# A two-layer graph network on one core: eleven counted groups move from layer 0 to the end of it and into layer 1

## The chip, the core and the metric

The kernel runs on one core of a Trainium2 chip. Its engines run side by side, each through its own list of instructions, and meet at semaphores: PE (TensorE) multiplies matrices into PSUM, DVE (VectorE) and ACT (ScalarE) work on elements, POOL (GpSimd) and SP (SyncE) issue DMAs, and ACT issues some too. The metric is the device time of one execution in microseconds (us); less is better.

## The reference

There are 6250 nodes with 128 features and 100000 edges, sorted by their destination. One layer, applied twice, is

```python
msg = (h[src] + edge_feats) @ Wn.T
agg = segment_sum(msg, dst, num_segments=num_nodes)
agg = agg / maximum(deg, 1.0)[:, None]
self_msg = where(iso[:, None], h @ Wi.T, h @ Ws.T)      # iso = deg == 0
x = agg + self_msg
h_next = where(x >= 0, x, RRELU_SLOPE * x)
```

Both layers have the same edges and edge features, and weights of their own. The result is the layer norm of `x + h` over the features.

## The kernel before, in words

The sum over a node's edges is taken before the product with `Wn`. The edges stand in 784 chunks of 128. Four chunks are a window, whose destinations lie within 40 columns; 16 chunks are a group, whose destinations lie within 136. There are 196 windows and 49 groups. The layer's sums lie in SBUF as `sums`, features by nodes.

*Edge features* are needed once: layer 1 starts from layer 0's sums, and adds only the difference that `h` makes. They are loaded window by window (SP, five windows ahead) and multiplied with a one-hot matrix `onehot` of the destinations, into `ps_win`. In two windows of five DVE first splits the features into three bf16 parts (`split_feats`), and PE multiplies three times in bf16 in place of once in f32.

*Source rows* `h[src]` come in one of two ways.
- Gathered: POOL issues one indirect DMA per chunk, in order, up to five windows (`ROWS`) ahead of PE (`gather`). PE multiplies the three bf16 parts of the rows with the one-hot matrix. All windows of groups that are not counted go this way.
- Counted: for a group, a matrix `counts` (nodes by 136 columns) says how often each node is the source of an edge into each column. It is multiplied with all nodes' parts `h_parts`: 49 tiles x 3 parts = 147 products. To make it, DVE writes for each chunk two one-hot matrices, `is_lane` and `is_code` (`make_codes`), six chunks ahead (`AHEAD`); PE multiplies them into a bank of `ps_count`, in two pieces of 294 and 343 columns and a small one of 49 (`count_piece`); ACT copies each piece from PSUM into one of three buffers of `counts` (`keep_chunk`).

32 of the groups are `KEEPABLE`; 31 of these are `KEPT`, counted for layer 1. 20 of the 31 are `USED`: counted in layer 0 too. The other 11 are gathered in layer 0, and counted only for layer 1. So in layer 0 two groups in three are gathered, but one in three where a second group is `USED` (the 7th, 19th, 31st and 43rd).

*Order.* Layer 0 runs in beats of one window. The plan `plan_layer0` deals two used groups and one other, and says how many chunks are counted in each beat and which tiles of a used group are multiplied. A full buffer is stored to DRAM by SP (`store_counts`, 1764 KB), for layer 1. `count_piece` goes round three banks, and waits for ACT's copy of the piece three before.

After a beat in which three groups are summed, a node step follows for 384 nodes: the products with the three weights, the activation, and `h` split into parts and stored in `h_parts_rows`. When all steps are through, SP loads `h_parts` back in seven cuts of seven tiles (`load_parts`), and POOL begins layer 1's gathers.

Layer 1 also runs in beats of a window: 72 windows are gathered. SP loads the 31 stored counts in seven cuts each, 217 loads of 252 KB, up to 21 ahead (`load_counts`). Per beat PE multiplies three or four cuts ("pieces", 21 products each, `multiply_kept`), then its window, then what is due of node steps. DVE adds the group's sums (`take_dense`) and the window's, and ACT stores the results.

The rows name what the products write: `ps_count` L1246 and L1250 are counts being made, `ps_dense` L1258 groups of layer 0 multiplied, `ps_count` L1258 those of layer 1 (they use the banks of `ps_count`), `ps_win` L1197 windows, `ps_self` L1310 and `ps_node` L1323 node steps.

Of the kernel before, what the change touches and what calls it, by code (L numbers as in the profile page):

```python
# [5 lines left out]
def plan_layer0(kept, used, beats, buffers, per_chunk, tiles, tiles_per_beat, head):  # L6
# [10 lines left out]
    total = len(jobs) * per_chunk  # L17
    builds, pieces, built = [], [], 0
    build_beat, done_beat = {}, {}
    waiting = [j for j, g in enumerate(jobs) if g in used]  # L20
    k, tile = 0, 0
    while built < total or waiting:
        now = []
        while len(now) < 4 and built < min(total, head + (k + 1) * (total - head) // beats):
            j = built // per_chunk
            if j >= buffers and jobs[j - buffers] in used and done_beat.get(j - buffers, k) >= k:
# [7 lines left out]
        if waiting and build_beat.get(waiting[0], k) < k:  # L34
            j = waiting[0]
            cut = (j, tile, min(tiles, tile + int((k + 1) * tiles_per_beat) - int(k * tiles_per_beat)))
            tile = cut[2]
            if tile == tiles:
                done_beat[j] = k
                waiting.pop(0)  # L40
# [3 lines left out]
    return jobs, builds, pieces, build_beat, done_beat  # L44


def gnn_resnorm_kernel(nc, x_rows, x_cols, src, dst, edges, wn0, ws0, wi0, wn1, ws1, wi1, out):
# [51 lines left out]
    JOBS, BUILDS, MULTIPLIED, BUILT_BEAT, DONE_BEAT = plan_layer0(KEPT, USED, 188, BUFFERS, GC, TILES, 5.6, 8)  # L99
    USED_JOBS = [j for j, g in enumerate(JOBS) if g in USED]  # L100
    FIRST_COL = {g: i * GC for i, g in enumerate(KEEPABLE)}
    COUNTED = len(KEEPABLE) * GC
    LAST_MULTIPLY = max(DONE_BEAT.values())

# [11 lines left out]
    PIECES = len(KEPT) * CUTS  # L116
    SPREAD = len(ORDER1) - GW
    PIECES1 = [min(PIECES, k * PIECES // SPREAD) for k in range(len(ORDER1) + 1)]


    READY = [[], []]
    for u in range(TRIOS):
# [5 lines left out]
        pieces = CUTS * sum(g < 3 * u + 3 for g in KEPT)  # L128
# [31 lines left out]
    with ctx:  # L160
# [108 lines left out]
        counts_loaded = [sem(f"counts_loaded{i}") for i in range(BUFFERS * CUTS)]  # L269
# [89 lines left out]
        def dense_bank(nth):  # L359

            if nth < len(USED):
                return ps_dense[:, 0, 0:WIDE]
            return ps_count[:, (nth - len(USED)) % BANKS, 0:WIDE]
# [14 lines left out]
        def _(sp):  # L378
# [59 lines left out]
            def load_counts(q):  # L438

                i, cut = divmod(q, CUTS)  # L440
                if q == 0:
                    sp.wait_ge(group_multiplied, len(USED))
                    for b in range(BUFFERS):
                        sp.wait_ge(counts_stored[b], 16 * len(JOBS[b::BUFFERS]))
# [3 lines left out]
                sp.dma_start(counts[:, i % BUFFERS, t, :].rearrange("p t s -> p (t s)"),  # L448
                             counts_kept[FIRST_COL[KEPT[i]] // GC, :, CUT * cut * SPAN:CUT * (cut + 1) * SPAN]
                             ).then_inc(counts_loaded[q % (BUFFERS * CUTS)], 16)  # L450
# [3 lines left out]
            with sp.If(flag == 0):  # L454
                cuts = list(range(CUTS))
                for k in range(BEATS[0]):
# [7 lines left out]
                    for j in range(len(JOBS)):  # L464
                        if BUILT_BEAT[j] == k - 1:
                            store_counts(j)
                    while cuts and k > max(LAST_MULTIPLY, WINDOWS) and (
                            READY[0][min(-(-P * (1 + CUT * (cuts[0] + 1)) // TRIO), TRIOS) - 1] + 7 <= k):
                        load_parts(cuts.pop(0))
                for q in range(CUTS):  # L470
                    load_counts(q)
# [3 lines left out]
                for q in range(CUTS, PIECES):  # L475
                    load_counts(q)
# [79 lines left out]
        def _(dve):  # L556
# [332 lines left out]
            def layer0():  # L889
# [9 lines left out]
                for k in range(BEATS[0]):  # L899
                    for j in USED_JOBS:  # L900
# [21 lines left out]

            def layer1():
# [5 lines left out]
                for k in range(1, BEATS[1]):  # L929
                    while added < PIECES1[min(k, len(ORDER1))] // CUTS:  # L930
                        dve.wait_ge(cut_multiplied, CUTS * (added + 1))
# [13 lines left out]
                    node_stage1(k)  # L945
# [523 lines left out]
```

## Time and profile before

| | |
|---|---|
| median of 3 runs | 1080.71 us (1080.55 to 1085.12) |
| the profiled execution | 1087.57 us, its span 1085.8 us |
| busy: PE, DVE, ACT, POOL | 933.4, 691.7, 513.5, 760.0 us |
| layer 0's gathers by POOL | 442, busy 450.9 us |
| layer 1's gathers by POOL | 286, busy 278.1 us |
| stores of counts | 31 of 1764 KB |
| loads of counts | 217 of 252 KB |
| mean granted TensorE clock | 0.960 |

The span runs from the profile's first instruction to the last. "Busy" of PE is the union of modelled times from start to end; products overlap, so what one costs in a stream is read from start to start. An instruction's idle time before it stands in brackets with what ended it; "issue" means that the engine waited for nothing that the profile shows.

### The profile page before, as it was taken

What the parts mean: (1) busy time and instruction counts of PE and PEld (TensorE: products, weight loads), DVE (VectorE), ACT (ScalarE), POOL (GpSimd) and SP (SyncE); (2) the same over time, 40 slices, a digit from 0 to 9 for tenths busy, and PEclk for the clock granted to TensorE, in tenths of its full rate; (3) what the DMA queues carried; (4) which work ended last, traced back from release to release, by engine and by line L of the source; (5) the groups of instructions that cost most, each with busy time, mean ns of one, the idle gap of its engine ahead of it and who ended that gap; (6) DMA issues with size and microseconds to landing.
All of it is one profiled execution on the core that took longest, in us unless ns stands there. A gap on an engine that the chain in (4) does not pass through costs nothing.

```text
span 1085.8 us, 38527 instructions
## 1 busy us (share of the span) xinstructions
PE 933.4 (86%) x14592; PEld 869.7 (80%) x14592; DVE 691.7 (64%) x2388; ACT 513.5 (47%) x1143; POOL 760.0 (70%) x757
## 2 busy tenths in 40 slices
PE   1599989899998998998889987479999999999982
PEld 0488888788988887887878886479999999998981
DVE  7878987898897898887878885312243233423333
ACT  6478777777887777776767774100000000000000
POOL 8367757777767777767777657077777777777772
PEclk9999999999999999998989998599999999999995
DMA  9468877878887797797778778799988898888741
GB/s 303 154 198 269 298 250 261 268 258 277 278 287 260 241 325 249 225 314 243 230 231 282 250 253 298 225 367 316 281 260 271 252 280 273 262 265 276 225 117 52
DMA packets 154041, 277.50 MB, mean 256 GB/s; under 512 B 21458, under 2 KB 112572, under 8 KB 149884
## 3 DMA queue, kind: packets, MB, share of 16 engines
q1 hardware_dynamic: 93504, 184.10, 50.5%
q0 software_dynamic: 35584, 72.92, 22.9%
q10 hardware_dynamic: 24764, 17.95, 5.2%
q8 instruction: 120, 1.97, 0.7%
q14 instruction: 69, 0.57, 0.2%
HBM read 202.58 MB, written 72.30 MB: 253 GB/s over the span
## 4 chain that ended last, share of the span: by engine, by line
PE 48%; issue 6%; DVE 4%; DMA 3%; ACT 2%; POOL 2%; ACTq 1%; DVEq 0%; SPq 0%; POOLq 0%
PE ps_count L1258 25%; PE ps_win L1197 7%; PE ps_dense L1258 6%; PE ps_count L1246 5%; PE ps_self L1310 3%; PE ps_node L1323 2%; POOL rows L512 2%; DMA rows<-x_parts_rows,idx 1%; ACT counts L1051 1%; DVE is_code L727 1%; DMA counts<-counts_kept 1%; PE ps_win L1204 1%; DMA h_parts_rows<-row_parts 1%; DVE is_lane L725 1%; PE ps_self L1292 0%
## 5 line engine op out<-in xcount | busy, mean ns | idle before, releaser
L512 POOL DMA_INDIRECT rows<-x_parts_rows,idx x442 | 450.9, 1020 | 189.0 <-issue 127.9
L1051 ACT CAST counts<-ps_count 128x294 f32 x992 | 436.4, 504 | 151.2 <-PE ps_count L1246 69.1
L512 POOL DMA_INDIRECT rows<-h_parts_rows,idx x286 | 278.1, 972 | 111.9 <-issue 84.8
L1246 PE MATMUL ps_count<-is_code,is_lane 128*128 128x294 bf16 x992 | 301.9, 311 | 35.3 <-ACT counts L1051 33.4
L1258 PE MATMUL ps_dense<-counts,h_parts 128*128 128x136 bf16 x2940 | 311.0, 224 | 3.9 <-DVE sums L760 2.2
L1258 PE MATMUL ps_count<-counts,h_parts 128*128 128x136 bf16 x4557 | 282.1, 223 | 10.0 <-DMA counts<-counts_kept 10.0
L1258 PEld LDWEIGHTS ps_count<-counts,h_parts 128*128 128x128 bf16 x4557 | 273.5, 98 | 10.7 <-DMA counts<-counts_kept 10.4
L1197 PE MATMUL ps_win<-onehot,feats 128*128 128x40 f32 (+1 forms) x1564 | 245.0, 236 | 22.9 <-DVE sums L738 11.3
L1258 PEld LDWEIGHTS ps_dense<-counts,h_parts 128*128 128x128 bf16 x2940 | 210.2, 98 | 39.7 <-ACT counts L1051 5.1
L1197 PEld LDWEIGHTS ps_win<-onehot,feats 128*128 128x128 f32 (+1 forms) x1564 | 205.9, 158 | 28.1 <-issue 19.9
L727 DVE TENSOR_SCALAR is_code<-codes,code 128x637 bf16<-128x637 f16 x496 | 197.9, 399 | 0.0
L1197 PE MATMUL ps_win<-onehot,rows 128*128 128x40 bf16 (+1 forms) x2224 | 149.0, 186 | 32.4 <-issue 29.6
L738 DVE TENSOR_TENSOR sums<-sums,ps_win 128x80 f32 (+1 forms) x268 | 59.1, 220 | 184.0 <-PE ps_win L1197 134.1
L1063 ACT COPY self_sums<-ps_self 128x384 f32<-128x384 f32 (+1 forms) x34 | 16.1, 475 | 321.7 <-PE ps_self L1310 321.7
L1197 PEld LDWEIGHTS ps_win<-onehot,rows 128*128 128x128 bf16 (+1 forms) x2224 | 130.3, 112 | 36.5 <-issue 33.4
L725 DVE TENSOR_SCALAR is_lane<-column,lane 128x128 bf16<-128x128 bf16 x496 | 135.9, 274 | 36.7 <-PE ps_count L1250 34.7
L1246 PEld LDWEIGHTS ps_count<-is_code,is_lane 128*128 128x128 bf16 x992 | 108.3, 110 | 46.1 <-ACT counts L1051 40.5
L1250 PE MATMUL ps_count<-is_before,is_lane 128*128 128x49 bf16 x465 | 88.7, 191 | 0.0
L697 DVE TENSOR_TENSOR onehot<-column,rel 128x160 f32<-128x160 bf16 x268 | 84.8, 318 | 1.6 <-issue 1.6
L712 DVE TENSOR_TENSOR feats<-feats_rest 128x512 bf16<-128x512 f32 x78 | 58.4, 749 | 2.7
L710 DVE TENSOR_TENSOR feats_rest<-feats 128x512 f32<-128x512 f32 x78 | 53.2, 682 | 6.6 <-DMA feats<-in_edges_dram 6.5
L1197 PE MATMUL ps_win<-onehot,feats_rest 128*128 128x40 bf16 x310 | 56.0, 182 | 0.0
(99 smaller groups left out, 784.7 us busy)
## 6 DMA issues: line engine op xcount, KB each, us to landing
counts_kept<-counts SPq DMA_DIRECT2D x31, 1764.0 KB
counts<-counts_kept SPq DMA_DIRECT2D x217, 252.0 KB, 4.4
feats<-in_edges_dram SPq DMA_DIRECT2D x196, 256.0 KB
rows<-x_parts_rows,idx POOLq DMA_INDIRECT x442
x_parts_rows<-h_parts SPq DMA_DIRECT2D x7, 672.0 KB, 7.7
h_parts<-h_parts_rows SPq DMA_DIRECT2D x7, 672.0 KB, 9.6
h_parts_rows<-row_parts ACTq DMA_DIRECT2D x16, 288.0 KB
rows<-h_parts_rows,idx POOLq DMA_INDIRECT x286
```

The costliest lines, as they stand in the source:

```text
L512: nc.gpsimd.indirect_dma_start(rows[:, SUB * slot + c, :], None, table[:, :], bass.IndirectOffsetOnAxis(ap=indices[:, c:c + 1], axis=0)).t ...
L697: nc.vector.tensor_tensor(onehot[:, h:h + SUB, :], column[:, 0:W].unsqueeze(1).to_broadcast([P, SUB, W]), rel[:, chunk:chunk + SUB].unsque ...
L710: nc.vector.tensor_tensor(rest, f, upper(f), ALU.subtract).then_inc(feats_rest_made, 1)
L712: nc.vector.tensor_tensor(lower(f), rest, upper(rest), ALU.subtract).then_inc(feats_split, 1)
L725: nc.vector.tensor_scalar(is_lane[:, n % (AHEAD + 1), :], column[:, :], lane[:, col:col + 1], None, ALU.is_equal)
L727: nc.vector.tensor_scalar(is_code[:, n % AHEAD, :], codes[:, :], code[:, col:col + 1], None, ALU.is_equal).then_inc(codes_ready, 1)
L738: return nc.vector.tensor_tensor(s, s, p, ALU.add)
L1051: nc.scalar.copy(counts[:, j % BUFFERS, :, at(offset + first, count)], ps_count[:, q % BANKS, 0:count * TILES].rearrange("p (r t) -> p t r ...
L1197: last = nc.tensor.matmul(ps[:, 0, SUM * w:(SUM + 1) * w], left, right, start=first and i == 0, stop=final and i == len(lefts) - 1)
L1246: last = nc.tensor.matmul(ps[:, 0:count * TILES], is_lane[:, n % (AHEAD + 1), :], is_code[:, n % AHEAD, first * TILES:(first + count) * TI ...
L1250: last = nc.tensor.matmul(ps[:, 0:TILES], is_lane[:, (n - 1) % (AHEAD + 1), :], is_before[:, (n // 4) % 3, n % 4, :], start=False, stop=True)
L1258: last = nc.tensor.matmul(bank, h_parts[:, t, k, :], counts[:, b, t, 0:WIDE], start=(t == 0 and k == 0), stop=(t == TILES - 1 and k == PAR ...
```

## The change

The eleven groups that only layer 1 uses leave the middle of layer 0. Jobs are ordered by `USED` first, then `LATE`. `plan_layer0` now plans the 20 used groups over 176 beats (before, 31 over 188). Two late groups are counted right after the last used one, two chunks per beat, until beat 191. The other nine are counted in layer 1, three chunks a beat at most, by a new plan `plan_layer1`. The late groups are not stored and not loaded: they lie in two buffers of `counts`, and are multiplied from there. The third buffer (`RING`) takes the 20 stored groups, one after another: 140 loads in place of 217; a cut is loaded when the same cut of the group before is multiplied. From the first late group on, counts are made in two banks of `ps_count`; the third bank and `ps_dense` take layer 1's groups in turn. Layer 1 begins with 14 pieces before its first window (before, three): two groups' first six cuts, then their last. The first seven loads are issued when the last features are. `SPLIT_RATE`, two windows in five, is the same number before and after.

```diff
-    plain = [g for g in kept if g not in used]
-    jobs, first = [], list(used)
-    while first or plain:
-        for some, count in ((first, 2), (plain, 1)):
-            jobs += some[:count]
-            del some[:count]
...
+def plan_layer1(order, late, built, beats, first, per_chunk, most):
+    chunks = late * per_chunk
+    ends, done, builds, upto, pos = {}, {}, [], [0], 0
+    for p in range(built // per_chunk):
+        ends[p] = -1
+    k = 0
+    while pos < len(order) or built < chunks:
+        target = first + max(0, (len(order) - first) * k // beats)
+        while pos < min(target, len(order)):
+            p, last = order[pos]
+            if p is not None and ends.get(p, k) >= k:
+                break
+            if p is not None and last:
+                done[p] = k
+            pos += 1
+        upto.append(pos)
+        now = []
+        while len(now) < most and built < chunks:
+            p = built // per_chunk
+            if p >= 2 and done.get(p - 2, k) >= k:
+                break
+            now.append(built)
+            built += 1
+            if built % per_chunk == 0:
+                ends[p] = k
+        builds.append(now)
+        k += 1
+    return upto, builds
...
-    JOBS, BUILDS, MULTIPLIED, BUILT_BEAT, DONE_BEAT = plan_layer0(KEPT, USED, 188, BUFFERS, GC, TILES, 5.6, 8)
+    LATE = [g for g in KEPT if g not in USED]
+    JOBS = USED + LATE
+    BUILDS, MULTIPLIED, BUILT_BEAT, DONE_BEAT = plan_layer0(len(USED), 176, BUFFERS, GC, TILES, 5.6, 8)
...
-    PIECES1 = [min(PIECES, k * PIECES // SPREAD) for k in range(len(ORDER1) + 1)]
+    PIECES = [(i, c) for i in range(2) for c in range(CUTS - 1)] + [(i, CUTS - 1) for i in range(2)]
+    PIECES += [(i, c) for i in range(2, len(KEPT)) for c in range(CUTS)]
...
+    PIECES1, BUILDS1 = plan_layer1(
+        [(LATE.index(KEPT[i]) if KEPT[i] in LATE else None, c == CUTS - 1) for i, c in PIECES],
+        len(LATE), 2 * GC, len(ORDER1) - GW, 2 * CUTS, GC, 3)
...
+    COUNT_BANK = [q % BANKS if q < LATE_COUNTS else q % 2 for q in range(COUNTS)]
...
-                if q >= BUFFERS * CUTS:
-                    sp.wait_ge(cut_multiplied, q - BUFFERS * CUTS + 1)
+                if l >= CUTS:
+                    sp.wait_ge(cut_multiplied, LOADED[l - CUTS] + 1)
...
+                    if k == max(LAST_MULTIPLY + 2, WINDOWS - FEATS):
+                        for l in range(CUTS):
+                            load_counts(l)
...
+            def make_late_codes(k):
+                for n in (BUILDS1[k] if k < len(BUILDS1) else ()):
+                    if n + AHEAD < len(JOBS) * GC:
+                        make_codes(n + AHEAD)
...
+                if j >= len(USED) + 2:
+                    act.wait_ge(cut_multiplied, LAST_PIECE[KEPT.index(JOBS[j - 2])] + 1)
...
                 for k in range(BEATS[1]):
+                    keep_chunks(BUILDS1[k] if k < len(BUILDS1) else ())
                     if (1, "self", k) in STAGE:
...
-                    while k < len(ORDER1) and q < PIECES1[k + 1]:
-                        multiply_kept(q)
-                        q += 1
+                    builds = BUILDS1[k] if k < len(BUILDS1) else []
+                    q, q1 = (2 * builds[0], 2 * (builds[-1] + 1)) if builds else (0, 0)
+                    s, s1 = PIECES1[min(k, len(ORDER1))], PIECES1[min(k + 1, len(ORDER1))]
+                    while q < q1 or s < s1:
+                        if q < q1:
+                            count_piece(q)
+                            count_piece(q + 1)
+                            q += 2
+                        if s < s1:
+                            multiply_piece(s)
+                            s += 1
```

In PE's list, at the end of layer 0's last node step (`ps_node<-ident`) and the start of layer 1, there stood before (L1258 are pieces, x63 three of them, L1197 a window):

```order
L1310 MATMUL ps_self<-wts,h_in 128x128
L1323 MATMUL ps_node<-wts,sums 128x128 x2
L1333 MATMUL ps_node<-ident,h_row 128x128 x2
L1258 MATMUL ps_count<-counts,h_parts 128x136 x63
L1197 MATMUL ps_win<-onehot,rows 128x40 x12
```

and now (L1341 are pieces, L1280 a window, L1329 counts being made):

```order
L1412 MATMUL ps_node<-wts,sums 128x128 x2
L1422 MATMUL ps_node<-ident,h_row 128x128 x2
L1341 MATMUL ps_dense<-counts,h_parts 128x136 x126
L1341 MATMUL ps_count<-counts,h_parts 128x136 x126
L1341 MATMUL ps_dense<-counts,h_parts 128x136 x21
L1341 MATMUL ps_count<-counts,h_parts 128x136 x21
L1280 MATMUL ps_win<-onehot,rows 128x40 x12
L1329 MATMUL ps_count<-is_code,is_lane 128x294
L1329 MATMUL ps_count<-is_code,is_lane 128x343
L1341 MATMUL ps_dense<-counts,h_parts 128x136 x21
```

Fourteen pieces moved ahead of the first window, and from the second beat on a chunk is counted ahead of each piece.

In SP's list, from the last features to layer 1's loads, there stood before (L426 stores counts, L435 loads h's parts, L448 loads counts):

```order
L426 DMA counts_kept<-counts 128x7056
L387 DMA feats<-in_edges_dram 128x512 x2
L414 DMA h_in<-in_x_cols_dram 128x256
L421 DMA x_trio<-in_x_rows_dram 128x2x128
L435 DMA h_parts<-h_parts_rows 128x7x384 x6
L448 DMA counts<-counts_kept 128x1008 x7
L435 DMA h_parts<-h_parts_rows 128x7x384
L384 DMA wts<-in_wn_dram 128x128
```

and now (L512 loads counts, L498 h's parts):

```order
L450 DMA feats<-in_edges_dram 128x512 x2
L512 DMA counts<-counts_kept 128x1008 x7
L477 DMA h_in<-in_x_cols_dram 128x256
L484 DMA x_trio<-in_x_rows_dram 128x2x128
L498 DMA h_parts<-h_parts_rows 128x7x384 x7
L447 DMA wts<-in_wn_dram 128x128
```

The store ahead of the last features is gone, and the seven loads of counts moved from behind h's parts to the place right behind the last features, ahead of the last node step's inputs.

## Rows read from the trace of the kernel before

**Rows 1.** Groups of POOL's instructions: busy us, mean ns | idle before.

```profile
L512 POOL DMA_INDIRECT rows<-x_parts_rows,idx x442 | 450.9, 1020 | 189.0 <-issue 127.9 <-PE ps_win L1204 61.1
L512 POOL DMA_INDIRECT rows<-h_parts_rows,idx x286 | 278.1, 972 | 111.9 <-issue 84.8 <-DMA h_parts_rows<-row_parts 25.0 <-PE ps_win L1197 2.1
```

**Rows 2.** Timeline of POOL (start us, us): each layer's first and last gather.

```profile
51.50 0.94 POOL L512 DMA_INDIRECT rows<-x_parts_rows,idx  x1 [13.35 <-PE ps_win L1204]
...
677.16 0.95 POOL L512 DMA_INDIRECT rows<-x_parts_rows,idx  x1 [0.30 <-issue]
703.13 0.94 POOL L512 DMA_INDIRECT rows<-h_parts_rows,idx  x1 [25.02 <-DMA h_parts_rows<-row_parts]
...
1067.15 0.95 POOL L512 DMA_INDIRECT rows<-h_parts_rows,idx  x1 [0.30 <-issue]
```

**Rows 3.** Two stretches: us, POOL busy (gathers), PE clock, DMA share, GB/s.

```profile
200.00:250.00 50.00, 38.41 (x39) 1.00 0.85 291
...
600.00:650.00 50.00, 28.12 (x27) 1.00 0.74 242
```

**Rows 4.** Groups of PE between 100 and 600 us, the larger count.

```profile
L1246 PE MATMUL ps_count<-is_code,is_lane 128*128 128x343 bf16 x395 | 125.3, 317 | 29.2 <-ACT counts L1051 28.7
```

**Rows 5.** Timeline of PE at the end: last window, last node product.

```profile
1070.47 0.36 PE L1197 MATMUL ps_win<-onehot,rows 128*128 128x40 bf16 x6 [2.94 <-issue]
...
1074.76 1.19 PE L1323 MATMUL ps_node<-wts,sums 128*128 128x128 f32 x4 [2.05 <-DVEq L944]
```

**Rows 6.** Timeline of PE in layer 0, counts among products.

```profile
400.99 0.29 PE L1246 MATMUL ps_count<-is_code,is_lane 128*128 128x294 bf16 x1
401.12 0.34 PE L1258 MATMUL ps_dense<-counts,h_parts 128*128 128x136 bf16 x3
401.29 0.31 PE L1246 MATMUL ps_count<-is_code,is_lane 128*128 128x343 bf16 x1
...
401.46 0.34 PE L1258 MATMUL ps_dense<-counts,h_parts 128*128 128x136 bf16 x3
```

**Rows 7.** Timeline of ACT in layer 0, six copies.

```profile
662.78 2.47 ACT L1051 CAST counts<-ps_count 128x294 f32 x6 [0.58 <-PE ps_count L1246]
```

**Rows 8.** Timeline of POOL and DVE, gathers beside DVE's work.

```profile
400.30 0.95 POOL L512 DMA_INDIRECT rows<-x_parts_rows,idx  x1 [0.30 <-issue]
...
400.45 0.38 DVE L727 TENSOR_SCALAR is_code<-codes,code 128x637 bf16<-128x637 f16 x1
...
402.51 0.68 DVE L710 TENSOR_TENSOR feats_rest<-feats 128x512 f32<-128x512 f32 x1
...
402.81 1.21 POOL L512 DMA_INDIRECT rows<-x_parts_rows,idx  x1 [0.31 <-issue]
```

**Rows 9.** Timeline between the layers: parts and counts issued, PE's first piece.

```profile
687.53 9.61 SPq L435 DMA_DIRECT2D h_parts<-h_parts_rows  x6
...
697.32 4.80 SPq L448 DMA_DIRECT2D counts<-counts_kept  x7
...
705.44 5.36 PE L1258 MATMUL ps_count<-counts,h_parts 128*128 128x136 bf16 x63 [9.96 <-DMA counts<-counts_kept]
```

**Rows 10.** Timeline of PE in layer 1: starts give each kind's cost.

```profile
1033.66 0.47 PE L1310 MATMUL ps_self<-wts,h_con 128*128 128x128 f32 x2
...
1035.08 3.89 PE L1258 MATMUL ps_count<-counts,h_parts 128*128 128x136 bf16 x63
...
1038.81 0.46 PE L1197 MATMUL ps_win<-onehot,rows 128*128 128x40 bf16 x12
1039.11 3.89 PE L1258 MATMUL ps_count<-counts,h_parts 128*128 128x136 bf16 x63
...
1043.14 0.91 PE L1323 MATMUL ps_node<-wts,sums 128*128 128x128 f32 x6
...
1043.89 3.89 PE L1258 MATMUL ps_count<-counts,h_parts 128*128 128x136 bf16 x63
```

**Rows 11.** DMA issues: KB each, median us to landing.

```profile
counts<-counts_kept SPq DMA_DIRECT2D x217, 252.0 KB, 4.4
```

More of the change, by code:

```diff
@@ L3, with plan_layer0 @@
 from contextlib import ExitStack
-def plan_layer0(kept, used, beats, buffers, per_chunk, tiles, tiles_per_beat, head):
-    plain = [g for g in kept if g not in used]
-    jobs, first = [], list(used)
-    while first or plain:
-        for some, count in ((first, 2), (plain, 1)):
-            jobs += some[:count]
-            del some[:count]
-    total = len(jobs) * per_chunk
+def plan_layer0(jobs, beats, buffers, per_chunk, tiles, tiles_per_beat, head):
+    total = jobs * per_chunk
     builds, pieces, built = [], [], 0
     build_beat, done_beat = {}, {}
-    waiting = [j for j, g in enumerate(jobs) if g in used]
-    k, tile = 0, 0
-    while built < total or waiting:
+    k, job, tile = 0, 0, 0
+    while built < total or job < jobs:
         now = []
@@ L25, in plan_layer0 @@
             j = built // per_chunk
-            if j >= buffers and jobs[j - buffers] in used and done_beat.get(j - buffers, k) >= k:
+            if j >= buffers and done_beat.get(j - buffers, k) >= k:
                 break
@@ L33, in plan_layer0 @@
         cut = None
-        if waiting and build_beat.get(waiting[0], k) < k:
-            j = waiting[0]
-            cut = (j, tile, min(tiles, tile + int((k + 1) * tiles_per_beat) - int(k * tiles_per_beat)))
+        if job < jobs and build_beat.get(job, k) < k:
+            cut = (job, tile, min(tiles, tile + int((k + 1) * tiles_per_beat) - int(k * tiles_per_beat)))
             tile = cut[2]
             if tile == tiles:
-                done_beat[j] = k
-                waiting.pop(0)
+                done_beat[job] = k
+                job += 1
                 tile = 0
@@ L103, in gnn_resnorm_kernel @@
     LAST_MULTIPLY = max(DONE_BEAT.values())
+    late_chunk, k = len(USED) * GC, BUILT_BEAT[len(USED) - 1] + 1
+    while late_chunk < (len(USED) + 2) * GC:
+        late = late_chunk // GC
+        if k == len(BUILDS):
+            BUILDS.append([])
+        while len(BUILDS[k]) < 2 and late_chunk < (late + 1) * GC and DONE_BEAT[late - BUFFERS] < k:
+            BUILDS[k].append(late_chunk)
+            late_chunk += 1
+        k += 1
     ORDER0 = [(3 * u + i, j) for u in range(STEPS) for j in range(GW) for i in range(3)]
@@ L127, in gnn_resnorm_kernel @@
         beat = sum(g < 3 * u + 3 for g, j in ORDER1)
-        pieces = CUTS * sum(g < 3 * u + 3 for g in KEPT)
+        pieces = max([LAST_PIECE[i] + 1 for i, g in enumerate(KEPT) if g < 3 * u + 3])
         beat = max(beat, next(k for k, q in enumerate(PIECES1) if q >= pieces))
@@ L268, in gnn_resnorm_kernel @@
         counts_stored = [sem(f"counts_stored{i}") for i in range(BUFFERS)]
[L269 removed]
+        counts_loaded = [sem(f"counts_loaded{i}") for i in range(CUTS)]
         group_multiplied = sem("group_multiplied")
@@ L474, in _ @@
                 load_weights(1)
-                for q in range(CUTS, PIECES):
-                    load_counts(q)
+                for l in range(CUTS, len(LOADED)):
+                    load_counts(l)
             with sp.Else():
@@ L899, in layer0 @@
                 for k in range(BEATS[0]):
-                    for j in USED_JOBS:
+                    for j in range(len(USED)):
                         if DONE_BEAT[j] == k - 1:
@@ L1050, in keep_chunk @@
                         act.wait_ge(piece_kept, q - 1)
-                    nc.scalar.copy(counts[:, j % BUFFERS, :, at(offset + first, count)],
-                                   ps_count[:, q % BANKS, 0:count * TILES].rearrange("p (r t) -> p t r", t=TILES)
+                    nc.scalar.copy(counts[:, buffer_of(j), :, at(offset + first, count)],
+                                   ps_count[:, COUNT_BANK[q], 0:count * TILES].rearrange("p (r t) -> p t r", t=TILES)
                                    ).then_inc(piece_kept, 1)
@@ L1119, in load_next_x, with keep_chunks @@
                 act.dma_start(by_row(x_trio[:, 0:real(u) * D]), by_tile(x_rows[trio_cols(u), :])).then_inc(x_loaded, 16)
+            offsets = []
+            def keep_chunks(chunks):
+                for n in chunks:
+                    if n % GC == 0:
+                        begin_job(n // GC)
+                        offsets[:] = load_offsets(JOBS[n // GC])
+                    keep_chunk(n, offsets[n % GC])
             def layer0():
```

101 lines of the change are left out of this document (59 added, 42 removed).

## The prediction

> **What bounds the kernel now.** I read the groups of instructions of GpSimd (POOL) first. In both layers it issues one gather after another: 442 for layer 0, busy 450.9 us, and 286 for layer 1, busy 278.1 us [rows 1]. Layer 0's run goes from 51.50 to 678.11 us, layer 1's from 703.13 to 1068.10 [rows 2]. Two gathers are never less than 0.30 us apart ("issue" in the rows). So layer 0's run of 626.6 us holds 450.9 us of gathers, 441 x 0.30 = 132.3 us between them, and 43.4 us in which POOL stood still for TensorE (PE). Layer 1's holds 278.1 + 285 x 0.30 = 363.6 of 365.0: POOL never stops there and sets layer 1's length.
>
> The stretches come next: in 200 to 250 us POOL makes 39 gathers, in 600 to 650 only 27 [rows 3]. A full POOL makes one in (450.9 + 132.3) / 442 = 1.32 us. It is therefore full in ordinary stretches and runs into its five-window limit only where one group in three is gathered rather than two. PE sets the pace in layer 0, but POOL is 43 us behind it as a bound.
>
> The lines of PE between 100 and 600 us show that PE also waits: 28.7 us before the larger count product, for ScalarE (ACT), which copies the piece out of PSUM [rows 4].
>
> The end of the timeline shows layer 1's bound: before its last window PE waits 2.94 us for the gather [rows 5], and so before the two ahead of it.
>
> **Layer 0: 144 chunks fewer.** Of 496 chunks 352 stay (20 jobs of 16, and two late jobs in beats 176 to 191). Start to start, a chunk takes 0.13 us for the 294 columns and 0.17 for the 343 and 49, 0.30 in all [rows 6]. PE so loses 144 x 0.30 = 43.2 us. ACT's copies take 2.47 / 6 = 0.41 us each [rows 7]: 288 x 0.41 = 118 us less, and with that the reason for most of PE's 28.7 us of waiting per 500. VectorE loses 144 pairs of codes, of 0.38 us for the larger [rows 8]. Eleven of 31 stores of counts go too; no engine's wait is put down to one, and I count them at nothing.
>
> PE could save 43 us of work and some 20 to 30 of waiting, together more than the 43.4 us that POOL has to spare. So POOL becomes the bound and caps the gain. A little of its standing still must remain: the first beats still build four chunks each, and in the first special stretch (from about 150 us) POOL still starts with a full lead. I leave 9 us for these and take **-34 us**. Bounds: -46 (all 43.4, and gathers a little shorter with less work on VectorE), and -15 (PE keeps its present waits and a third of its saved work reaches the end).
>
> The splitting of features costs nothing: two in five windows were split before, 78 of 196 both times; a few move by a beat or two.
>
> **Between the layers.** The last store of counts leaves SP's queue; instead the seven loads of layer 1's first job stand behind the last features. They wait only for stores long done. So the last windows' gathers still share the DMA engines with one transfer of a whole job: no change. SP then still waits for the last node step, and issues h's parts where it does now, at 687.53 [rows 9]. Before, seven loads of counts followed at 697.32, and PE began at 705.44, when the first landed [rows 9]. Now the counts are there, and PE can begin as parts land. Counted in before's time: SP needs 9.6 us to issue six parts, so I let PE begin at 697, and multiply 14 pieces before its first window. A piece is 21 products, 3.73 / 3 = 1.24 us [rows 10]; 14 are 17.4 us, and some 3 more for the half clock that PE has here. It is then at 717, an estimate. The first window's four gathers are issued by 708 (703.13 and four times 1.28), so they are there.
>
> **Layer 1.** From 717 PE has 203 pieces x 1.24 = 252; 71.5 windows x 0.30 = 21.5; node products, (1.42 + 0.75) x 16.7 trios = 36 [rows 10]; and new, 144 chunks x 0.30 = 43. Sum 353, and so PE ends at 1070 if nothing stops it. Before, its last product ran at 1074.8 after waits for gathers [rows 5]. PE and POOL are now almost equal: POOL's last gather at 1068.1 stays, PE has lost its slack.
>
> What stops it: a count pair needs its two banks back. ACT needs 2 x 0.41 = 0.82 us for a pair, and a piece of 1.24 us always stands between two pairs, so normally nothing. Where ACT clears a new job's tail (nine times) or waits for the normalization (17 times) I allow half a microsecond each, 26 x 0.5 = 13, of which a half shows. VectorE has the codes made two beats ahead. The counted groups that are loaded now have one buffer: a load is issued when the same cut of the group before is multiplied, six pieces (7.5 us) ahead; landing took 4.4 us [rows 11], so it is hidden. If that cover went, 133 loads could cost what they are late.
>
> So PE reaches the end 1070 + 7 = 1077 against 1074.8, and some unevenness between two engines that are equally loaded adds a little: **+5 us**, bounds -2 (the last store of h's parts lands earlier without seven loads beside it) and +25 (all the 13 us, and POOL slowed as below).
>
> **What VectorE's codes do to the gathers.** In layer 1 a gather took 0.972 us, in layer 0, with VectorE busy, 1.020 [rows 1]. The gather at 400.30 took 0.95 us with a code product beside it at 400.45; that at 402.81 took 1.21, beside the two subtractions of the feature split [rows 8]. By these rows the codes are harmless, the two-input operations are not, and these stay in layer 0. The sum has nothing for it. The Trainium skill, SBUF — State Buffer, section "SBUF: two separate sides", says that VectorE and GpSimd hold a shared pair of ports exclusively, one blocking the other, and names VectorE's two-port modes and its operations with two SBUF inputs. If the codes run in such a mode, they too would slow the gathers by that rule; the 0.95 us beside one speaks against it, the 1.21 us agrees with the half on two inputs. What it would do here is the second rival.
>
> **Sum.** -34 + 5 = -29 us. The profiled execution took 1087.57 us (span 1085.8); 1058.6 is left. The median of the runs is 1080.71, 0.63% under the profiled one; in the same proportion **1052 us**.
>
> **Rivals.**
> - PE does not catch POOL. If ACT's and VectorE's turns keep half of the saving from the end, layer 0 gives 17 instead of 34: 1069. For it: PE's waits are spread over many partners. Against: ACT loses over a third of its copies. Chance 0.14.
> - POOL slows in layer 1, as codes and gathers meet there. At layer 0's duration: 286 x (1.020 - 0.972) = 13.7 us on a POOL that has no slack; POOL ends at 1081.8, 9 us behind the forecast's layer 1: 1061. Chance 0.12.
> - Both ends go well: layer 0 gives all 43 and layer 1 costs nothing: 1038. Chance 0.10.
> - Slower: in layer 1 PE and ACT fall into lockstep. With two banks in place of three, each late copy stops the next pair, and nothing but one piece lies between. From 29 / 144 = 0.20 us per chunk the gain is gone; at one copy in full, 0.41 us, it is 59 us: 1052 + 59 = 1111. For it: PE already waits for these copies with three banks and fewer products between. Against: the 0.82 against 1.24 us above. Chance 0.07.
>
> The forecast has 0.57. Within 0.5% of the time before (1075.3 to 1086.1), about what a measurement can tell from no change, fall a part of the first rival and the mild end of the last: 0.08. Slower 0.06, faster 0.86. The range in which I expect the time is 1036 to 1071: it holds the first three rivals but for their ends.
>
> **What the profile will show.** Right: POOL's run in layer 0 some 590 us long with almost no wait for PE, 39 gathers per 50 us everywhere; layer 1's run still 365 us; PE's wait for counts between the layers gone, and 14 pieces before its first window; PE at its full clock with no waits at the end. Wrong: POOL still waiting 20 us or more in layer 0; count pairs in layer 1 with a wait for ACT before them (lockstep); POOL waiting for PE's windows in layer 1 by more than a few us; waits for the loaded counts in the runs of three or four loaded groups.

## The result: a half per cent faster, where 2.7% was forecast

In twenty runs each, the changed kernel takes 1077.37 us (median; 1068.32 to 1083.73), the kernel before 1082.07 (1079.72 to 1087.7): ratio 0.9945, interval 0.9924 to 0.9966. A second set gave 0.9928, 0.9904 to 0.9952. By the ratios that is 6 to 8 us where the forecast had 29, and the time lies above the range given.

The profiled execution took 1072.14 us (span 1070.3), 5 us under its median, while the profiled one of before lay 5 above its later median: the pair would show 15 us. So I compare two profiled executions of each kernel. The table is worked out from POOL's rows in the traces: start of a layer's first gather to the end of its last, and for layer 1 also to the end of the span.

| us | before, two executions | after, two executions | difference of means | forecast |
|---|---|---|---|---|
| layer 0's gathers | 626.6, 625.8 | 591.6, 600.9 | -30.0 | -34 |
| of which POOL stands still beyond its 0.30 us gaps | 43.4, 41.6 | 12.5, 24.0 | | 9 left |
| last gather of layer 0 to first of layer 1 | 25.0, 24.9 | 23.1, 23.4 | -1.7 | 0 |
| layer 1's gathers | 365.0, 363.3 | 383.7, 386.3 | +20.9 | 0 |
| layer 1's first gather to the end | 382.7, 381.4 | 405.0, 408.2 | +24.6 | +5 |

The three terms sum to -7.1 us, and the medians differ by 4.7 and 6.9. Layer 0 gave nearly what was forecast; layer 1 gave it back.

The groups of POOL's instructions after (columns as in [rows 1]):

```profile
L577 POOL DMA_INDIRECT rows<-x_parts_rows,idx x442 | 446.8, 1011 | 158.1 <-issue 125.0 <-PE ps_win L1287 33.1
L577 POOL DMA_INDIRECT rows<-h_parts_rows,idx x286 | 279.3, 977 | 127.6 <-issue 86.0 <-DMA h_parts_rows<-row_parts 23.1 <-PE ps_win L1280 18.5
```

Against [rows 1], the wait for PE in layer 0 fell from 61.1 to 33.1 (both hold the 13.35 before the first gather), and in layer 1, where POOL waited 2.1 us before, it now waits 18.5. The first and last gathers, against [rows 2]:

```profile
50.53 0.94 POOL L577 DMA_INDIRECT rows<-x_parts_rows,idx  x1 [13.35 <-PE ps_win L1287]
...
640.96 1.18 POOL L577 DMA_INDIRECT rows<-x_parts_rows,idx  x1 [0.30 <-issue]
665.28 0.94 POOL L577 DMA_INDIRECT rows<-h_parts_rows,idx  x1 [23.14 <-DMA h_parts_rows<-row_parts]
...
1048.09 0.95 POOL L577 DMA_INDIRECT rows<-h_parts_rows,idx  x1 [0.30 <-issue]
```

Three stretches, as in [rows 3] (POOL busy and gathers, PE's granted clock, DMA share, GB/s):

```profile
200.00:250.00 50.00, 38.42 (x39) 0.97 0.76 247
...
574.00:612.00 38.00, 26.29 (x27) 0.96 0.72 225
...
600.00:640.00 40.00, 28.31 (x29) 0.83 0.74 222
```

and the last 40 us of layer 0's gathers in the kernel before:

```profile
636.00:676.00 40.00, 28.30 (x29) 0.94 0.84 280
```

The second stretch holds the same 27 gathers (the 394th to the 420th) as the 50 us in [rows 3]. From the first start to the last they take 37.6 and 40.6 us in the two executions after, 48.6 and 47.3 before; at POOL's full rate of 1.32 us it would be 34. The last 40 us hold 29 gathers in both kernels, so nothing was gained there; PE's clock is granted at 0.83 in them, 0.94 before. PE's larger count product, against [rows 4], waits 7.1 us for ACT, not 28.7:

```profile
L1329 PE MATMUL ps_count<-is_code,is_lane 128*128 128x343 bf16 x289 | 91.4, 316 | 8.4 <-ACT counts L1127 7.1 <-issue 1.2
```

Between the layers the timeline goes nearly as forecast. Against [rows 9], the wait for loaded counts is gone and PE begins 9.5 us ahead of POOL's first gather (forecast 6); its first window runs 13.2 us after that gather (forecast 13.9):

```profile
649.76 15.14 SPq L498 DMA_DIRECT2D h_parts<-h_parts_rows  x7
...
655.82 6.09 PE L1341 MATMUL ps_dense<-counts,h_parts 128*128 128x136 bf16 x63
...
678.51 0.46 PE L1280 MATMUL ps_win<-onehot,rows 128*128 128x40 bf16 x12
```

**Where layer 1 lost it.** The waits from 690 to 1070 us (engine and line, what it waited for: us in total, times, longest):

```profile
DVE rstd L921 <- ACT std L1167: 65.7, 16, 6.8
...
POOL rows L577 <- PE ps_win L1280: 18.2, 15, 3.2
ACT counts L1127 <- DVE h_rest L926: 13.8, 8, 1.8
PE ps_count L1329 <- ACT counts L1127: 12.9, 9, 3.3
```

The same view of the kernel before has the first pair too, 2.1 us of the second, and none of the last two; there POOL set the pace, and VectorE's wait cost next to nothing:

```profile
DVE rstd L856 <- ACT std L1091: 55.6, 10, 7.5
```

After the change the four pairs are links of one chain: VectorE waits for ACT's root, ACT's copies wait for VectorE's normalization (`h_rest` L926), PE's counts wait for ACT's copies, POOL waits for PE's windows. The timeline shows one such stop (start, us; weight loads and other work left out):

```profile
863.77 0.47 PE L1399 MATMUL ps_self<-wts,h_con 128*128 128x128 f32 x2
...
865.20 0.43 PE L1329 MATMUL ps_count<-is_code,is_lane 128*128 128x294 bf16 x2
...
865.40 0.48 ACT L1139 COPY self_sums<-ps_self 128x384 f32<-128x384 f32 x1 [10.89 <-PE ps_self L1399]
...
865.47 1.41 PE L1341 MATMUL ps_dense<-counts,h_parts 128*128 128x136 bf16 x21
865.79 0.30 ACT L1167 ACTIVATE std<-mv,eps 128x3 f32<-128x3 f32 x1
...
866.33 0.86 DVE L926 TENSOR_SCALAR h_rest<-h_rest,mv,rstd 128x128 f32<-128x128 f32 x3
...
867.22 0.40 ACTq L1172 DMA_DIRECT2D out_dram<-h_rest  x1
...
867.65 0.68 ACT L1116 COPY counts<-zeros 128x588 f32<-128x588 f32 x1 [1.57 <-DVE h_rest L926]
...
869.38 0.88 ACT L1127 CAST counts<-ps_count 128x294 f32 x2 [1.04 <-issue]
...
870.11 0.52 PE L1329 MATMUL ps_count<-is_code,is_lane 128*128 128x294 bf16 x2 [3.24 <-ACT counts L1127]
```

ACT's list in such a beat is: the beat's counts, the copy of the next trio's self products, the root for this trio, the store of its result. The self products are PE's last work of the beat, so ACT waits for the beat's end (865.37). Only then comes the root (865.79), VectorE normalizes (866.33 to 867.19), and ACT waits for that before it issues the store. PE has long begun the next beat: the pair at 865.20 fills both banks, one piece follows, and then it stands 3.24 us until ACT has copied. Here a new group's tail is cleared in between as well. PE's last product is at 1058.95: 393.7 us after POOL's first gather, and 371.6 before ([rows 2, 5]).

### The profile page after: what moved, and what is told of

The parts are those of the page before. It is cut to its first block, busy times and chain, and to the rows that moved or that the text cites. A ratio compares the mean times of both kernels' runs of the same rounds, so it can differ in the third digit from the quotient of the medians.

```text
span 1070.3 us, 38440 instructions
## 1 busy us (share of the span) xinstructions
PE 942.5 (88%) x14592; PEld 880.3 (82%) x14592; DVE 696.6 (65%) x2388; ACT 534.1 (50%) x1143; POOL 756.2 (71%) x757
## 4 chain that ended last, share of the span: by engine, by line
PE 45%; POOL 8%; issue 6%; DVE 4%; DMA 3%; ACT 3%; ACTq 2%; SPq 1%; DVEq 0%; POOLq 0%
PE ps_dense L1341 16%; PE ps_count L1341 11%; POOL rows L577 8%; PE ps_count L1329 6%; PE ps_win L1280 6%; PE ps_self L1399 3%; DMA rows<-x_parts_rows,idx 2%; ACT counts L1127 2%; PE ps_node L1412 2%; DMA h_parts<-h_parts_rows 1%; DVE h_rest L926 1%; SPq L498 1%; ACTq L1102 1%; PE ps_win L1287 1%; PE ps_count L1333 1%
## 5 line engine op out<-in xcount | busy, mean ns | idle before, releaser
L1127 ACT CAST counts<-ps_count 128x294 f32 x992 | 456.8, 502 | 346.0 <-PE ps_count L1329 207.4
L1341 PE MATMUL ps_dense<-counts,h_parts 128*128 128x136 bf16 x5292 | 450.3, 226 | 11.4 <-DVE sums L825 7.2
L1341 PEld LDWEIGHTS ps_dense<-counts,h_parts 128*128 128x128 bf16 x5292 | 350.6, 99 | 44.8 <-issue 9.2
L1329 PE MATMUL ps_count<-is_code,is_lane 128*128 128x294 bf16 x992 | 285.5, 312 | 31.9 <-ACT counts L1127 27.2
L1280 PE MATMUL ps_win<-onehot,feats 128*128 128x40 f32 (+1 forms) x1564 | 253.4, 241 | 33.7 <-DMA rows<-x_parts_rows,idx 13.3
L1280 PEld LDWEIGHTS ps_win<-onehot,feats 128*128 128x128 f32 (+1 forms) x1564 | 212.7, 163 | 40.1 <-issue 25.5
L790 DVE TENSOR_SCALAR is_lane<-column,lane 128x128 bf16<-128x128 bf16 x496 | 138.4, 279 | 99.9 <-PE ps_count L1333 91.4
L1280 PE MATMUL ps_win<-onehot,rows 128*128 128x40 bf16 (+1 forms) x2224 | 150.4, 187 | 2.3 <-DVE sums L803 2.3
L1341 PE MATMUL ps_count<-counts,h_parts 128*128 128x136 bf16 x2205 | 144.6, 224 | 0.0
L1329 PEld LDWEIGHTS ps_count<-is_code,is_lane 128*128 128x128 bf16 x992 | 104.5, 111 | 39.9 <-issue 15.5
L1341 PEld LDWEIGHTS ps_count<-counts,h_parts 128*128 128x128 bf16 x2205 | 132.6, 98 | 3.3
L1280 PEld LDWEIGHTS ps_win<-onehot,rows 128*128 128x128 bf16 (+1 forms) x2224 | 132.9, 113 | 2.5 <-issue 2.4
L786 DVE TENSOR_TENSOR is_before<-column,before 128x196 bf16<-128x196 bf16 x124 | 44.4, 358 | 41.0 <-PE ps_count L1333 39.7
L1280 PE MATMUL ps_win<-onehot,feats_rest 128*128 128x40 bf16 x310 | 56.7, 183 | 0.0
```

The source lines that it names most:

```text
L786: nc.vector.tensor_tensor(is_before[:, (n // 4) % 3, :, :], column[:, 0:TILES].unsqueeze(1).to_broadcast([P, 4, TILES]), before[:, col:col ...
L790: nc.vector.tensor_scalar(is_lane[:, n % (AHEAD + 1), :], column[:, :], lane[:, col:col + 1], None, ALU.is_equal)
L1127: nc.scalar.copy(counts[:, buffer_of(j), :, at(offset + first, count)], ps_count[:, COUNT_BANK[q], 0:count * TILES].rearrange("p (r t) -> ...
L1280: last = nc.tensor.matmul(ps[:, 0, SUM * w:(SUM + 1) * w], left, right, start=first and i == 0, stop=final and i == len(lefts) - 1)
L1329: last = nc.tensor.matmul(ps[:, 0:count * TILES], is_lane[:, n % (AHEAD + 1), :], is_code[:, n % AHEAD, first * TILES:(first + count) * TI ...
L1341: last = nc.tensor.matmul(bank, h_parts[:, t, k, :], counts[:, b, t, 0:WIDE], start=(t == 0 and k == 0), stop=(t == TILES - 1 and k == PAR ...
```

## The experiments

Theory A was that this order of ACT's makes layer 1 long; rival B, that the single ring of loads or the lost third bank costs more still; rival C, that PE simply has too much to do. (The letters in the recorded expectations are each run's own.)

**Both kernels again** (labels r_before, r_after), for second profiles.

> The kernel before once more, for a second profile of it and the granted clock of each run. Theory A (the two profiled executions that were compared lie at opposite ends of their kernels' runs): its profiled time lies near 1082 us, not 1087, and layer 1's run of gathers still takes 365 us. Rival B (single executions stand for their kernel): 1087 again.

> The changed kernel once more, for a second profile and the clock of each run. Theory A: its time follows the granted clock; at 0.955 about 1077 us, and from the first gather of layer 1 to the end 400 to 410 us, against 383 before. Rival B: layer 1 is as long as before in the usual run, and the profiled execution showed a rare one.

Measured: before 1085.18 us, ratio to itself 1.0017 (0.9994 to 1.004); after 1076.72, ratio 0.9928. Their profiles are the second values in the table. The profiled execution of before, 1085.15 us, lies at that set's median, between the 1082 and the 1087 that were expected, and its layer 1 is as long as in the first; after's second profile lies at the top of its runs, with layer 1 at 408.2 us as Theory A had it. The two executions of after differ by 13.8 us in their span, and by their clock (core, span, mean granted clock); the first:

```profile
core 0: 1070.3 us, clock 0.962
```

and the second:

```profile
core 0: 1084.1 us, clock 0.948
```

If the clock stands at one of its two levels, 1.2 or 2.4 GHz, mean 0.948 is 113 us at the lower one and 0.962 is 81; half of the 32 between them is work not done, 16 us by estimate, about the difference. Whether the clock made the execution long or followed it, this doesn't show.

**The root first** (label e1_root_first, repeated as r_root_first). In ACT's loop of layer 1 (brackets shorten lines):

```diff
+                    if (1, "normalize", k) in STAGE:
+                        root(STAGE[1, "normalize", k])
                     keep_chunks(BUILDS1[k] if k < len(BUILDS1) else ())
-                    if (1, "self", k) in STAGE:
-                        (copy of the self products, next loads)
                     if (1, "normalize", k) in STAGE:
                         u = STAGE[1, "normalize", k]
-                        root(u)
                         (next load, store)
+                    if (1, "self", k) in STAGE:
+                        (copy of the self products, next loads)
```

> In layer 1 ScalarE takes the square root of a node step before the beat's counts, and stores the step right after them, ahead of the self products' copy. Theory A (ScalarE, held by the normalization, lets the count banks stand full, and PE waits some 15 us for them in layer 1): 10 to 16 us shorter than the changed kernel, and PE's waits for ScalarE before the counts of layer 1 under 4 us. Rival B (layer 1 is longer because PE has 43 us more to multiply, and the waits only fill what would be waits for gathers): within 4 us of the changed kernel.

> The kernel with ACT's new order in layer 1 once more, for a second profile of it. Theory A: layer 1 from POOL's first gather to the end 386 us, 20 less than in the kernel after; ratio 0.977 to 0.980.

Measured: 1060.07 us, ratio 0.9772 (0.9746 to 0.9798), 16.6 us under the changed kernel on the same chip; again, 1057.81 and 0.9746 (0.971 to 0.9782), a little under the 0.977 expected. Layer 1 from first gather to end: 385.9 us in both, 20.7 less than after. PE's waits for ACT from 690 us on:

```profile
PE ps_count L1330 <- ACT counts L1127: 2.6, 3, 0.9
```

and POOL's gathers there, whose wait for PE is back from 18.5 to 4.0:

```profile
L577 POOL DMA_INDIRECT rows<-h_parts_rows,idx x286 | 278.1, 972 | 109.8 <-issue 83.7 <-DMA h_parts_rows<-row_parts 22.2 <-PE ps_win L1281 4.0
```

The beat of the stop shown above, in the timeline of this kernel:

```profile
844.13 0.30 ACT L1167 ACTIVATE std<-mv,eps 128x3 f32<-128x3 f32 x1 [4.70 <-DVE mv L917]
...
845.73 0.92 DVE L926 TENSOR_SCALAR h_rest<-h_rest,mv,rstd 128x128 f32<-128x128 f32 x3
846.68 0.38 ACTq L1172 DMA_DIRECT2D out_dram<-h_rest  x1
...
850.12 0.43 PE L1330 MATMUL ps_count<-is_code,is_lane 128*128 128x294 bf16 x2
850.32 0.48 ACT L1139 COPY self_sums<-ps_self 128x384 f32<-128x384 f32 x1 [5.90 <-PE ps_self L1400]
...
850.71 0.68 ACT L1116 COPY counts<-zeros 128x588 f32<-128x588 f32 x1
851.93 0.88 ACT L1127 CAST counts<-ps_count 128x294 f32 x2 [0.53 <-issue]
852.66 0.52 PE L1330 MATMUL ps_count<-is_code,is_lane 128*128 128x294 bf16 x2 [0.86 <-ACT counts L1127]
```

Root, normalization and store lie 4 us ahead of the self copy; the stop is 0.86 us in place of 3.24. Theory A holds.

**Layer 1's counts left out** (label e2_no_late). The nine groups that layer 1 would count are not made; PE multiplies what lies in their buffers, with all loads and both banks as after.

```diff
-    BUILDS1 = [[len(USED) * GC + n for n in now] for now in BUILDS1]
+    BUILDS1 = []
...
-                    pe.wait_ge(piece_kept, 2 * GC * (j + 1))
+                    pe.wait_ge(piece_kept, 2 * GC * min(j + 1, len(USED) + 2))
```

> Layer 1's nine groups are not counted at all (144 chunks: no products, no copies, no codes; the two buffers keep the counts of the first two late groups). Theory A (the counts and their waits are the whole cost of the change in layer 1): POOL is the bound of layer 1 again, from its first gather to the end 380 us, so some 22 us shorter than the changed kernel, 1055. Rival B (the ring of one buffer, or the smaller number of banks, costs too): layer 1 stays over 388 us.

Measured: 1052.32 us, ratio 0.9697 (0.9666 to 0.9729); layer 1 380.6 us. POOL bounds again: it stands still for 1.4 us in all of layer 1, as before the change, and PE waits before its windows (the profile has no landing for gathers, and says "issue"):

```profile
PE ps_win L1280 <- issue: 37.3, 25, 4.1
```

The ring of loads costs nothing that shows. The lost third bank isn't tested here, since no counts are made; with the root first they are made in two banks, and layer 1 is only 5.3 us longer than in this run, so the two banks cost 5.3 us at most. Rival B falls with the two runs together. Rival C falls with the root first as well: PE has all its work there.

**The root ahead of the self copy, counts still first** (label e5_root_before_self), to part the two waits:

```diff
                     keep_chunks(BUILDS1[k] if k < len(BUILDS1) else ())
+                    if (1, "normalize", k) in STAGE:
+                        root(STAGE[1, "normalize", k])
                     if (1, "self", k) in STAGE:
                         (copy of the self products, next loads)
                     if (1, "normalize", k) in STAGE:
                         u = STAGE[1, "normalize", k]
-                        root(u)
```

> The kernel after, in whose layer 1 ACT takes the root for the normalization ahead of the copy of the next trio's self products, both still behind the beat's counts. ACT then still waits for the self products at the beat's end, but no more for VectorE's normalization after that, some 1.7 of the 3 us of a stop. Theory A1 (the two waits in a row make the stop, each by its part): stalls of PE in layer 1 from 20 us to 8, 1066. Rival A2 (the wait for the self products alone makes it): as the kernel after, 1077. Rival A3 (the normalization alone): as with the whole new order, 1060.

Measured: 1069.18 us, ratio 0.9876 (0.984 to 0.9912); layer 1 400.1 us. Of the 20.7 us between after and the whole new order this takes 6.5. The large stops remain, shorter (timeline of PE):

```profile
764.10 0.69 PE L1330 MATMUL ps_count<-is_code,is_lane 128*128 128x294 bf16 x2 [2.55 <-ACT counts L1127]
...
865.66 0.56 PE L1330 MATMUL ps_count<-is_code,is_lane 128*128 128x294 bf16 x2 [2.05 <-ACT counts L1127]
```

and ACT before the second of them:

```profile
862.13 0.48 ACT L1139 COPY self_sums<-ps_self 128x384 f32<-128x384 f32 x1 [5.92 <-PE ps_self L1400]
862.14 0.34 ACTq L1190 DMA_DIRECT2D h_in<-h_cols  x1
...
862.51 0.45 ACTq L1195 DMA_DIRECT2D x_trio<-in_x_rows_dram  x1
...
863.00 0.50 ACTq L1172 DMA_DIRECT2D out_dram<-h_rest  x1
863.54 0.68 ACT L1116 COPY counts<-zeros 128x588 f32<-128x588 f32 x1 [0.94 <-issue]
```

The same beat so stops 3.24 us after the change, 2.05 with the root ahead of the self copy, 0.86 with the whole new order. By these differences, of the 3.24, 1.2 are VectorE's normalization, waited for behind the self copy; 1.2 are the load and the store that ACT issues there, which I had not counted in my expectation; 0.86 are the self copy, one load and the clearing, which stay. A1 holds in kind, but its sizes were wrong: PE's stops in layer 1 fell from 19.9 us to 13.7 (intervals above 0.45 us, less 0.2 each), not to 8, and the normalization's share was 1.2, not 1.7.

**The same edit in the kernel before** (label e6_before_root_first), with the root ahead of the self copy and the store still behind it.

> The kernel before with the root ahead of the copy of the self products in layer 1, as in the run above. ACT copies no counts in layer 1 there, and POOL sets its length. Theory A: no change, ratio 0.998 to 1.002. Rival (the order is a gain by itself, whatever ACT has to copy): 0.985 to 0.99.

Measured: 1080.83 us against 1085.32, ratio 0.9972 (0.9951 to 0.9994), a little more than I expected; layer 1's gathers take 362.4 us (before 365.0 and 363.3), and 15.2 us follow them in place of 17.7 and 18.1. The trace settles what shortens that tail. In the kernel before, VectorE stands for the last but one root, which waits behind the self copy:

```profile
1073.35 0.18 DVE L856 RECIPROCAL rstd<-std 128x3 f32<-128x3 f32 x1 [4.96 <-ACT std L1091]
```

It adds the last window only after that, and PE's last node product waits 2.05 us for it [rows 5]. With the root first that product follows without a wait:

```profile
1066.99 1.06 PE L1324 MATMUL ps_node<-wts,sums 128*128 128x128 f32 x4
```

The gathers themselves are shorter (275.5 us busy, where they were 278.1 and 276.4); why stays open. So the order is a small gain by itself: 3.0 us by the ratio and 4.5 by the medians, a fifth to a quarter of what the whole new order gives the changed kernel. The rest needs an ACT that has counts to copy.

**More groups counted in layer 0**, on top of the new order (labels e3_used22, e7_used21, e4_used23). For 22:

```diff
-    USED = sorted([g for g in KEPT if g % 3 == 0] + [7, 19, 31, 43])
+    USED = sorted([g for g in KEPT if g % 3 == 0] + [7, 13, 19, 31, 37, 43])
...
-    ... plan_layer0(len(USED), 176, BUFFERS, GC, TILES, 5.6, 8)
+    ... plan_layer0(len(USED), 176, BUFFERS, GC, TILES, 6.2, 8)
```

21 adds the 25th alone, with 5.9; 23 adds the 13th, 25th and 37th, with 6.2.

> With ACT's new order, 22 groups used in layer 0 in place of 20 (the 13th and 37th too). POOL gathers 32 chunks fewer there, 32 x 1.31 = 42 us; PE gets two groups more to multiply, 2 x 147 products x 0.059 = 17 us, and counts 32 chunks more, 32 x 0.30 = 10, less 8 windows of products: +25 us. Theory A (in layer 0 the kernel after is bound by POOL, with PE some 10 to 35 us behind it as a bound): layer 0 gets shorter until PE is the bound, by 5 to 20 us; 1050 in place of 1060. Rival B (PE is bound in layer 0 too, so POOL's short idle is only the lead): 25 us longer, 1085. Rival C (PE has ample time): the whole 42 us, 1018.

> With ACT's new order, 21 groups used in layer 0 (the 25th too). POOL 16 x 1.31 = 21 us less, PE 8.7 + 4.8 - 1.2 = 12 us more. In layer 0 PE and POOL are both at their limit (22 groups: POOL 42 us less, PE 25 us more, and layer 0's gathers 19 us longer). Theory A: 6 to 12 us longer than with 20. Rival (there is an optimum between, at 21): 5 us shorter.

> As the kernel with 22 used groups, with the 25th used as well: POOL 21 us less once more, PE 12 us more. Theory A: PE is the bound by now in layer 0, POOL waits for it there by 20 us or more, and the time is 5 to 12 us above that with 22: about 1058. Rival C (PE still has time): 1018 - 21, under 1000.

| groups used | ratio to before | layer 0's gathers, us | of which POOL stands still, us |
|---|---|---|---|
| 20 (two runs) | 0.9772, 0.9746 | 589.2, 596.1 | 9.3, 15.3 |
| 21 | 0.9869 | 601.9 | 40.4 |
| 22 | 0.9843 | 608.5 | 68.7 |
| 23 | 0.9762 | 598.4 | 77.5 |

The idle sum of POOL's group in layer 0 shows it, for 22 groups (the wait for PE 91.4 us, where it was 31.7 with 20):

```profile
L577 POOL DMA_INDIRECT rows<-x_parts_rows,idx x410 | 417.1, 1017 | 204.7 <-issue 113.4 <-PE ps_win L1288 91.4
```

None of the three expectations held as stated. For 22 I had 1050, and it took 17 us more (1066.99). For 21 I had 6 to 12 us more than with 20, and it took 14.5 (1072.31 against 1057.81); by the profiles layer 0 is some 9 us longer and layer 1 7. There the first window runs 22.7 us after the first gather, not 12.9, and SP issues the seven loads of counts right ahead of h's parts; whether that is why, no run separates. For 23 the 1058 came (1059.32), but not its reason: it was to lie 5 to 12 us above 22, and lies 8 below.

What holds is that gathers saved on POOL turned into standing still there, for PE. How much room PE has in layer 0 stays open. By my sums of PE's work, the run with 21 leaves it 6 us at most (12 of work more, 6 to 13 longer), that with 22 leaves 6 to 13 (25 more, 12 to 19 longer), and that with 23 leaves 28 to 35 (37 more, 2 to 9 longer). These don't agree; the runs also change the plan's rate, and the clock of 23 was granted higher (0.973 in two of four runs). Layer 1 is shorter with fewer late groups, 382.0 and 382.4 us with 22 and 23, which is 3.5 of what makes 23 end no later than 20. The best that the runs found is 20 groups with the root first, and 23 is not clear of it.

## Why the prediction failed, by its own steps

- **Layer 0, -34 us:** measured -30.0 and, with the root first, -33.6 (mean of 589.2 and 596.1 against 626.2). Right in size, also that PE's waits for ACT go (28.7 to 7.1 us). Half right in its reason: POOL does not cap alone. Its standing still was 12.5 and 24.0 us, the second over the 20 I had named as a sign against me, and the runs with 21 to 23 groups show PE there as well. In the last 40 us of layer 0's gathers PE's clock is granted at 0.83, where it was 0.94 before, and PE has fewer products there, 495 against 539. The Trainium skill's page "TensorE: Matmul & The Clock Gate", Part 1, says that the throttled state is the default and activity releases it, and these rows agree. I had no term for that.
- **Between the layers, no change:** -1.7 us; PE's start came 3.4 us earlier against the first gather than worked out, its first window 0.7 earlier.
- **Layer 1, +5 us:** the failed step; it measured +24.6. Work was forecast at 353 us after the first window. From start to start, with intervals above 0.45 us cut to 0.2, it is 361, and the intervals cut off hold 19.9 more, where I had allowed 7. With the root first it is 355 and 7.2. So the sum of PE's work was sound; the sentence that fell is "a piece of 1.24 us always stands between two pairs, so normally nothing", with 13 us of allowances "of which a half shows". I had priced ACT's copies by their own 0.82 us and each other job by half a microsecond, and not followed ACT's list through one beat. There the copies stand behind two waits: for PE's last product of the beat and for VectorE. Before, both cost next to nothing (some 2 us at the end, as the run with the root first in the kernel before shows), since ACT had little other work in layer 1. Of the 8 us of work that came on top some 5.5 are gone with the root first; PE's clock is granted at 1.00 through layer 1's gathers with the root first, and at 0.99 with the stops. "VectorE has the codes made two beats ahead" fell too, at a smaller price: at 791.54 us PE stands 1.6 us for a code, after VectorE stood 5.66 us for the root.
- **The rivals.** What came is the slower rival's mechanism, PE and ACT in step with two banks, but not at every chunk: nine stops between 690 and 1070 us, three of them over 2.8 us. I had given it 0.07, with 59 us at one copy per chunk; its mild end, within half a per cent, is where the time fell. PE not catching POOL in layer 0 did not come. The fast rival did not either. The argument against the first, that ACT loses over a third of its copies, was wrong in size: 288 of 992 are 29%.
- **Codes beside gathers:** layer 1's gathers took 977 ns on average with codes made beside them, 972 before, 1.4 us in all against 13.7 of that rival. The price was rightly left out, but the reading that codes are harmless was wrong. Two codes and gathers, in the timeline of after:

```profile
681.41 0.38 DVE L792 TENSOR_SCALAR is_code<-codes,code 128x637 bf16<-128x637 f16 x1
681.52 1.09 POOL L577 DMA_INDIRECT rows<-h_parts_rows,idx  x1 [0.30 <-issue]
...
711.51 0.41 DVE L792 TENSOR_SCALAR is_code<-codes,code 128x637 bf16<-128x637 f16 x1
711.56 0.95 POOL L577 DMA_INDIRECT rows<-h_parts_rows,idx  x1 [0.30 <-issue]
```

Of layer 1's gathers with nothing of VectorE beside them but the making of codes (`is_lane`, `is_code`), 15 of 51 took over 1.00 us; of those with nothing beside them, none of 76. 14 of the 15 began 0.08 to 0.18 us behind a code, as the first above did, and ended 1.19 to 1.20 us after that code's start. A gather 0.05 us behind a code, or ahead of it like the one in [rows 8], was not slowed. And an operation with two inputs beside a gather, with the root first:

```profile
706.20 0.56 DVE L838 TENSOR_TENSOR h_in<-h_in,h_con 128x384 f32<-128x384 f32 x1
...
706.33 1.25 POOL L577 DMA_INDIRECT rows<-h_parts_rows,idx  x1 [0.30 <-issue]
```

The Trainium skill, "SBUF — State Buffer", section "SBUF: two separate sides", lets VectorE block GpSimd in a two-port mode, or with two SBUF inputs against a GpSimd operation that reads SBUF. The last pair of rows agrees with the part on inputs, and the first shows that a code can hold a gather up; whether the codes run in a two-port mode no run here shows.

- **The sum.** With the stops removed the three terms measure -33.6, -2.2 and +3.9 us (means of the two profiles with the root first), -32 against the -29 forecast, by profiles; by medians the two runs give 24 and 27 (1060.07 against 1083.61, 1057.81 against 1085.02), and their ratios 0.9772 and 0.9746 lie just above the 0.973 that 1052 stood for. One unread list of ACT's was the error.

## What to carry to other kernels

When work is given to an engine that was idle in a stage, write down that engine's instructions for one full turn in order, with what each waits for, and ask what stands behind the latest wait: waits that were free become the price of every instruction queued behind them. Put what others wait for ahead of what waits for others. And when two engines come out nearly equal in a sum, an allowance of half a microsecond per meeting is not a bound; the row that bounds it is the longest chain of waits in one turn.

## What was not expected of the hardware

One kernel's executions spread over 15 us (1068.32 to 1083.73) and its two profiled ones with their mean granted clock (0.962 and 0.948 for spans of 1070.3 and 1084.1 us), though the instructions are the same. In places the clock is granted lower, 0.83 over 40 us at the end of layer 0. Which comes first, the wait or the clock, these runs don't tell.
